# A recommendation tower on one core: the lookup matmuls of each unit are spread over three places, and the last block's tiles leave and return in turn

## The reference, cut to what matters

```python
e = jnp.stack([tbl_0[ids[:, 0]], ..., tbl_26[ids[:, 26]]], axis=1)   # 2048 x 27 x 128
dot = jnp.einsum('bnd,bmd->bnm', e, e)
z = dot.reshape(2048, 27 * 27)[:, lower_triangle]                    # 351 pairs
h = jnp.concatenate([z, dense_ctx], axis=1)
h = jnp.maximum(h @ W_top1 + b_top1, 0.0)
h = jnp.maximum(h @ W_top2 + b_top2, 0.0)
y = h @ W_top3
```

## Time and profile before

| | |
|---|---|
| median of 3 runs | 379.4 us (377.6 to 384.47) |
| profiled execution | 376.98 us, span 375.2 us, clock 0.973 |
| TensorE busy (weight loads) | 88% (81%) |
| VectorE, GpSimd, ScalarE busy | 67%, 67%, 36% |
| DMA | 46.39 MB, mean 124 GB/s |

### The profile page before, as it was taken

The page is one execution under the profiler, slowest core; times in us unless marked ns, Lnnn a source line. Parts: engine busy times, 40 slices in busy tenths (PEclk is TensorE's granted clock), DMA queues, the critical chain, the costliest instruction groups (busy, mean ns, idle before and its releaser), DMA issues.

```text
span 375.2 us, 14179 instructions
## 1 busy us (share of the span) xinstructions
PE 331.5 (88%) x6216; PEld 302.7 (81%) x6216; DVE 250.1 (67%) x757; ACT 134.3 (36%) x235; POOL 252.3 (67%) x271
## 2 busy tenths in 40 slices
PE   0776679788799999999999999999899999996786
PEld 0665679678699988998999988998799988995775
DVE  3899577697477669765876769666776769622031
ACT  2353424532222533333333343333233343344122
POOL 5777777777777777777777777777777777760000
PEclk9999698999899999999999999999999999999699
DMA  7999954248644665348544754447634755354410
GB/s 171 239 214 231 225 142 100 81 94 190 115 91 96 141 146 113 84 90 193 127 80 101 162 131 105 93 107 178 112 87 94 163 125 113 79 120 90 79 41 1
DMA packets 59215, 46.39 MB, mean 124 GB/s; under 512 B 38499, under 2 KB 53186, under 8 KB 59153
## 3 DMA queue, kind: packets, MB, share of 16 engines
q1 hardware_dynamic: 50705, 28.16, 35.0%
q0 software_dynamic: 8448, 17.32, 19.6%
HBM read 38.37 MB, written 7.09 MB: 121 GB/s over the span
## 4 chain that ended last, share of the span: by engine, by line
PE 62%; DMA 12%; POOL 11%; DVE 8%; issue 6%; ACT 1%; POOLq 0%
PE onehot_ps L593 16%; PE onehot_ps L595 13%; POOL rows L353 11%; PE dots_ps L621 10%; DMA idb<-ids_onehot 8%; DVE mask L494 7%; PE tile_ps L605 6%; PE mlp_ps L627 5%; PE mlp_ps L629 5%; PE mlp_ps L628 5%; DMA rows<-tbl,idx 3%; PE mlp_ps L662 2%; DMA idx<-ids_gather 1%; DVE z_lo L532 0%; DVE z_hi L529 0%
## 5 line engine op out<-in xcount | busy, mean ns | idle before, releaser
L353 POOL DMA_INDIRECT rows<-tbl,idx x264 | 251.5, 953 | 82.5 <-issue 79.6
L494 DVE TENSOR_SCALAR mask<-idb,cmp 125x256 fp32r<-125x256 int32 x672 | 208.8, 381 | 54.1 <-PE onehot_ps L595 32.2
L593 PE MATMUL onehot_ps<-mask,tab_hi 125*128 125x256 f32 x672 | 175.9, 300 | 28.5 <-DVE mask L494 17.6
L595 PE MATMUL onehot_ps<-mask,tab_lo 125*128 125x256 f32 x672 | 166.3, 284 | 0.0
L593 PEld LDWEIGHTS onehot_ps<-mask,tab_hi 125*128 125x128 f32 x672 | 129.6, 193 | 35.7 <-DVE mask L494 17.1
L595 PEld LDWEIGHTS onehot_ps<-mask,tab_lo 125*128 125x128 f32 x672 | 130.3, 194 | 0.0
L621 PEld LDWEIGHTS dots_ps<-emb 128*27 128x27 f32 x4096 | 45.4, 106 | 19.6 <-issue 16.4
L377 ACT COPY emb<-tile_ps 128x512 f32<-128x512 f32 x66 | 44.1, 671 | 46.9 <-PE tile_ps L605 45.4
L621 PE MATMUL dots_ps<-emb 128*27 128x27 f32 x4096 | 54.8, 194 | 6.3 <-issue 5.6
L368 ACT COPY emb<-onehot_ps 128x512 f32<-128x512 f32 (+1 forms) x46 | 36.3, 789 | 57.3 <-PE onehot_ps L595 54.7
L605 PE MATMUL tile_ps<-ident,rows 128*128 128x128 f32 x264 | 40.9, 279 | 4.5 <-DMA rows<-tbl,idx 4.5
(11 more groups left out here) (30 smaller groups left out, 153.0 us busy)
## 6 DMA issues: line engine op xcount, KB each, us to landing
idb<-ids_onehot SPq DMA_DIRECT2D x84, 128.0 KB
dots_dram<-dots SPq DMA_DIRECT2D x28, 216.0 KB
emb<-tbl SPq DMA_DIRECT2D x11, 448.0 KB
rows<-tbl,idx POOLq DMA_INDIRECT x264
zT<-dots_dram SPq DMA_DIRECT2D x14, 117.0 KB
dots_dram<-dots SPq DMA_DIRECT2D x8, 108.0 KB, 2.9
zT<-dots_dram SPq DMA_DIRECT2D x7, 104.0 KB
emb<-tbl SPq DMA_DIRECT2D x11, 52.0 KB
```

The source lines that it names most:

```text
L353: nc.gpsimd.indirect_dma_start(rows[:, n % RING, i, :], None, tables[feature][:, :], bass.IndirectOffsetOnAxis(idx[:, at:at + 1], 0)).then ...
L494: made = nc.vector.tensor_scalar(mask[0:VP, n % MASK_RING, c, :], idb[0:VP, k % IDB_RING, :], cmp[0:VP, at:at + 1], None, ALU.is_equal)
L593: nc.tensor.matmul(out, tab_hi[0:VP, f, at, :], mask[0:VP, k % MASK_RING, c, :], start=(at == 0), stop=False)
L595: done = nc.tensor.matmul(out, tab_lo[0:VP, f, at, :], mask[0:VP, k % MASK_RING, c, :], start=False, stop=(at == CHUNKS - 1))
```

## The change

On TensorE the parts of a unit no longer stand together behind the dots. The first two go between the transposes and the dots, the next two behind the dots, and the rest (two, or one) behind the unit's layers. ScalarE's list takes the same order. VectorE's list is as it was. Of the last block, tile 0 is stored, the dense part is loaded, and tile 0 is loaded back before tile 1 is stored. The sizes of the gather groups are written as functions, and a loop of loads is added.

```diff
-NGR_FIRST = NGR + len(LATE) // GROUP
+NGR_FIRST = NGR + 1
+def group_size(g):
+    return GROUP if g < NGR else len(LATE)
+GROUP_LIST = [(t, g) for t in range(NT) for g in range(groups(t))]
+GROUP_AT = [sum(group_size(g) for _, g in GROUP_LIST[:n]) for n in range(len(GROUP_LIST) + 1)]
+RING_USES = [sum(group_size(GROUP_LIST[k][1]) for k in range(n % RING, n + 1, RING)) for n in range(len(GROUP_LIST))]
+BEFORE_DOTS, BEFORE_LAYERS = 2, 4
+def pair_ends(f, h):
+    return h == PARTS - 1 and (f % 2 == 1 or f == NO - 1)
...
 @block.sync
+            for f in range(NO - NO_FIRST, IDB_RING):
+                load_idb(1, f)
             load_weights()
...
                 store_dots(LAST, q * P * half, dots[:, LAST % 2, q * half:(q + 1) * half], NQ // TILES,
                            last_out[q])
-            load_dense(LAST)
-            for q in range(TILES):
+                if q == 0:
+                    load_dense(LAST)
                 sp.wait_ge(last_out[q], 16 * QUAD)
                 load_z(LAST, q * P * half, slice(q * P, (q + 1) * P), NQ // TILES,
                        z_in if q == 0 else last_z_in)
...
 @block.scalar
+                    parts = unit_parts(u) if b < LAST else []
+                    for f, h in parts[:BEFORE_DOTS]:
+                        if pair_ends(f, h):
+                            empty_onehot(b + 1, f // 2)
                     empty_dots(b, u)
-                    if b < LAST:
-                        for f, h in unit_parts(u):
-                            if h == PARTS - 1 and (f % 2 == 1 or f == NO - 1):
-                                if b == 0 and f == 1:
-                                    act.wait_ge(lo_ready, NO)
-                                empty_onehot(b + 1, f // 2)
+                    for f, h in parts[BEFORE_DOTS:BEFORE_LAYERS]:
+                        if pair_ends(f, h):
+                            empty_onehot(b + 1, f // 2)
                     if b == 0 and u == 4:
                         split_w1_hi()
...
                         if u == LAYER2_AT:
                             relu2(b - 1)
+                    for f, h in parts[BEFORE_LAYERS:]:
+                        if pair_ends(f, h):
+                            empty_onehot(b + 1, f // 2)
...
 @block.tensor
+                    parts = unit_parts(u) if b < LAST else []
                     for g in GROUPS_AT[u % UNITS_TILE]:
                         if t < NT and g < groups(t):
                             tile_group(t, g)
+                    for f, h in parts[:BEFORE_DOTS]:
+                        onehot(b + 1, f, h)
                     dot_unit(b, u)
-                    if b < LAST:
-                        for f, h in unit_parts(u):
-                            onehot(b + 1, f, h)
+                    for f, h in parts[BEFORE_DOTS:BEFORE_LAYERS]:
+                        onehot(b + 1, f, h)
                     if b > 1 and u == LAYER3_AT:
                         layer3(b - 2)
...
                         if u == LAYER2_AT:
                             layer2(b - 1)
+                    for f, h in parts[BEFORE_LAYERS:]:
+                        onehot(b + 1, f, h)
```

More of the change, by code:

```diff
@@ L142, in build @@
         rows = sb("rows", [P, RING, GROUP, D], f32)
-        idx = sb("idx", [P, group(NT, 0) * GROUP], i32)
+        idx = sb("idx", [P, GROUP_AT[-1]], i32)
         idb = sb("idb", [P, IDB_RING, BLK], i32)
@@ L350, in _ @@
                         pool.wait_ge(tile_ps_full, n - RING + 1)
-                    for i in range(GROUP):
-                        feature, at = SLOTS[group_slot(g) + i], GROUP * n + i
+                    for i in range(group_size(g)):
+                        feature, at = SLOTS[group_slot(g) + i], GROUP_AT[n] + i
                         nc.gpsimd.indirect_dma_start(
@@ L365, in empty_onehot @@
             def empty_onehot(b, v):
+                if b == 1 and v == 0:
+                    act.wait_ge(lo_ready, NO)
                 a, z = 2 * v, min(2 * v + 2, looked_up(b))
@@ L376, in empty_group @@
                 act.wait_ge(tile_ps_full, n + 1)
-                nc.scalar.copy(samples[b % 2][:, q * P:(q + 1) * P, at:at + GROUP],
-                               tile_ps[:, n % 2, :].rearrange("p (k b) -> p b k", k=GROUP)
+                k = group_size(g)
+                nc.scalar.copy(samples[b % 2][:, q * P:(q + 1) * P, at:at + k],
+                               tile_ps[:, n % 2, 0:k * P].rearrange("p (k b) -> p b k", k=k)
                                ).then_inc(tile_ps_empty, 1)
@@ L602, in tile_group @@
                     pe.wait_ge(tile_ps_empty, n - 1)
-                pe.wait_ge(gathered[n % RING], 16 * GROUP * (n // RING + 1))
-                for i in range(GROUP):
+                pe.wait_ge(gathered[n % RING], 16 * RING_USES[n])
+                for i in range(group_size(g)):
                     done = nc.tensor.transpose(tile_ps[:, n % 2, i * P:(i + 1) * P], rows[:, n % RING, i, :],
@@ L734 @@
         "ids_gather": _np.stack([ids[t * P:(t + 1) * P, SLOTS[group_slot(g) + i]] for t in range(NT)
-                                 for g in range(groups(t)) for i in range(GROUP)], axis=1),
+                                 for g in range(groups(t)) for i in range(group_size(g))], axis=1),
         "ids_onehot": ids[:, ONEHOT].T,
```

## The result

The changed kernel takes 382.67 us (380.72 to 387.63, 20 runs) against 378.45 us (374.17 to 384.47, 20 runs) for the kernel before on the same chip: a ratio of 1.0139, 95% interval 1.0106 to 1.0172. That is 4.0 to 6.5 us, worked out on 378.45. The profiled execution took 380.77 us, 3.79 us more than before; its span is 379.0 us and its mean clock 0.973.

What follows compares the result with a forecast made beforehand. TensorE, just slower than the gathers, takes 41.7 us a block, set by VectorE and late ids. Terms +2.5 -1.0 -0.1 +0.4 +0 = +1.8 on 376.98 give 378.8, with 2.4 for the median 381.2 us; range 376 to 388.

Steps and rivals of the forecast that it cites:

- The sign and the place: Whole kernel: slower by +1.8 us in sum, with the largest term, +2.5, in block 0.
- Block 0, +2.5 (2.0 to 3.4): Block 0: dots no longer fill TensorE's mask waits, so weight splits, masks and the first store come later; 2.5 us taken.
- up to 1.0: Block 0: longer waits in units 5 and 6 may bring TensorE's granted clock down, adding up to 1.0 us.
- Five cycles, -1.0: Middle blocks, unit 7 to unit 7: layer 1 ahead of the fifth part brings ids earlier, 0.2 us gained in each of five.
- T: End of unit 6's last layer-1 product, taken to start the chain of masks, stores and ids; ids arrive at T + 18.83.
- Change-overs, 0: TensorE within each unit: transposes to lookups saves 0.1 us, lookups to dots costs 0.1; sum 0, bounds -1.5 to about +2.
- Block 6 to 7, +0.4: Start of block 7, which has no lookups as cover: TensorE waits 0.4 us for the copy of the last pair.
- Tail, 0: Last block's tiles: last loads start some 1.5 us earlier, but TensorE is held by block 6's layers until 363.2; 0 us.
- Tile 1's stores wait some tenths at most: SyncE's queue, last block: tile 0's loads fit into idle time ahead, so tile 1's stores behind them wait only some tenths.
- the cover: Tail: block 6's layers hold TensorE until 363.2, hiding when the last loads come; without it a gain of 1.5 us.
- Rival (b): Each block's store is released by the last dots' copy instead of mask 43: up to 5.6 us, 386.8 us; chance 0.13.
- Rival (a): Middle blocks: ids stop being late, TensorE waits for no mask; 6.7 us, capped by gathers at -3.6; 377 us, chance 0.13.

Runs made afterwards that it cites:

- e3: The change's lookup order in all blocks but block 0, last block's tiles as before, against the kernel before: 378.91 against 379.23 us, ratio 1.0012.
- e10: The change's lookup order in block 0 alone, later blocks and tiles as before, against the kernel before: 382.70 against 380.97 us, ratio 1.008.
- e5: Two parts ahead of the dots, all others between dots and layers, tiles as before, against the kernel before: 381.61 against 378.21 us, ratio 1.0106.
- the spread kernels: The four kernels with the change's lookup order throughout block 0, the changed kernel among them; mean granted clock 0.923 over 47 to 92 us.
- the old ones: The six kernels with block 0's lookups in the old order, the kernel before among them; mean granted clock 0.973 over 47 to 92 us.
- e8: The changed kernel with tiles as before and unit 7 of block 0 having its dots first, against the kernel before: 381.49 against 378.21 us, ratio 1.0134.
- e6: The kernel before with feature 4's ids issued ahead of the wait for the dots' stores to land: 373.27 against 378.21 us, ratio 0.9895.
- e2: The changed kernel's lookup order alone, last block's tiles as before, against the kernel before: 383.85 against 379.23 us, ratio 1.0102.
- e1: The kernel before with only the exchange of the last block's tiles: 379.84 against 379.23 us, ratio 1.0077.

## Why the prediction was right, and where its terms were not

The forecast of 381.2 us, no change that can be told, held: 382.67, though the interval of the ratio is clear of 1. The sign and the place were right. The effect was forecast at +1.8 us and is +4.0 to +6.5 by the ratio, +3.8 in the profile; what is missing is the gain of the middle blocks, half a microsecond each in block 0 and in the tail, and by the ratio 0.2 to 2.7 us more that no trace places. That the forecast time came within 1.5 us is in part luck: the kernel before came out 0.95 us lower here (378.45) than in the three runs shown, which hides part of what the sum lacks.

*Block 0, +2.5 (2.0 to 3.4).* The mechanism was right in the main: e3 and e10 show that block 0 carries the loss, and e5 that the two parts ahead of the dots move the store. Of the steps, the wait of unit 5 was to end 1.4 us later and that of unit 6 2.0. Counted from the end of unit 2's wait they came 16.95 us behind it for 15.55, +1.40, and 24.53 for 22.09, +2.44; but unit 2's own wait ended 1.56 us earlier (52.56 for 54.12), so against the span's start they are 0.16 earlier and 0.88 later. The store moved by 3.25, inside the forecast 2.0 to 2.4 with up to 1.0 of clock. In the one pair of profiles the term is 2.43; over all traces it is 2.8 to 3.5, and 3.0 by e10's ratio. It was sized about half a microsecond low. The forecast gave the clock "up to 1.0"; by the means over 47 to 92 us the spread kernels lose some 2.3 us more to it than the old ones, while this one pair of profiles shows no difference (0.96 both).

*Five cycles, -1.0.* Not borne out. What it rests on was seen in part: waits for z_lo of 0.51 to 0.97 us in unit 3 of three blocks of the six, no mask waits in that unit but one of 1.65 us in unit 2 of block 3, and middle stores 3.6 to 3.8 us behind T (3.63 before), that of block 5 here, with T = 291.77:

```profile
295.52 3.85 SPq L286 DMA_DIRECT2D dots_dram<-dots  x4
```

Leaving out the one late cycle of each, the mean is 41.30 us after and 41.41 before, 0.1 us for the 0.2 forecast. But one late arrival of the ids costs some 2 us, and five cycles sum to 208.38 to 213.66 us over eleven traces without the early ids, before, after and experiments mixed. The scatter is wider than the term.

*Change-overs, 0.* Right in both parts: lookups to dots 0.21 us, the same as ahead of layer 3, and the transposes' step to lookups 313.29 - 312.93 = 0.36 where the dots followed after 0.53, with 0.20 for the first lookup in place of 0.117.

*Block 6 to 7, +0.4.* The wait measured 0.41.

*Tail, 0.* The sum was about right, the steps were wrong. The last loads were to come 1.5 us earlier. "Tile 1's stores wait some tenths at most" failed: tile 0's loads wait for their stores to land until 353.91 and are 2.87 us long, so tile 1's stores start 2.27 us behind the copy that they need. A wait for z_lo of 0.38 us stands in place of the cover, and from TensorE's first layer-1 product of block 6, behind all the dots (354.69 now, 351.45 before), to the end is 26.08 us for 25.53, +0.55. The Trainium skill (DMA: Bandwidth & Descriptors, "Rules for kernel authors") would have work issued early and waited for late, and the forecast's estimate by that page's fixed cost was 2 us; the traces agree in the direction, with 0.6 to 1.3 us on the loads and 0.2 to 0.4 on the path.

*Rival (b)* did not happen in the middle blocks: the store of block 5 starts at 295.52, and the last copy of dots ends at 295.09. In block 0 it did, as the row at 84.92 shows; what undoing the dots' move there would give back, e8 can't tell. *Rival (a)*'s mechanism is real and e6 reaches it by another way: with the ids in time five cycles shrink by 6.2 us, and as the gathers bind behind them, 4.0 us of it are left by the ratio and 2.9 in the profiles, about its cap of 3.6. (Its 6.7 us for five cycles should read 6.5: 208.52 less 5 x 40.4.)

## What to carry to other kernels

Independent work put ahead of a short step lengthens no busy time, but it uses up the cover of the next wait. Here that showed in the first block, whose delay went on through a store. When all waits of a repeated block trace back to one transfer, look what the queue stands waiting for just ahead of it: moving that one issue gained 1.05% where moving the matmuls gained nothing. Before a term of 0.2 us a block is trusted, look how far the same interval scatters from block to block. And a clock read in one short window can favour the explanation it was chosen for: here only the window over the whole block showed that the kernel before had its low stretch too.

## What the runs showed of the hardware that was not expected

TensorE stops for some two microseconds in a dense row of small matmuls. These are the last dots of block 7 in the timeline of after, 128 matmuls and their 128 weight loads a row, with "issue" as the releaser (the kernel before shows the same, with 2.46 and 2.58 us):

```profile
346.70 1.37 PE L647 MATMUL dots_ps<-emb 128*27 128x27 f32 x128 [0.73 <-issue]
350.25 1.42 PE L647 MATMUL dots_ps<-emb 128*27 128x27 f32 x128 [2.18 <-issue]
353.98 0.78 PE L647 MATMUL dots_ps<-emb 128*27 128x27 f32 x46 [2.31 <-issue]
```

The granted clock is no plain function of the last wait: in 70 to 74 us it stayed at 1.00 behind 2.48 us (after) and stood at 0.64 behind 2.10 (e2), and in 74 to 78 us it stood at 0.62 behind a wait of 1.59 us for a gather, which ended at 73.58 (e1).
